# Local block: the feed-forward's layer norm on token rows, with transposes there and back

## The chip, the cores and the metric

The kernel runs on one core of a Trainium2 chip. The metric is the time of one execution on the device, in microseconds (us), the median of several. "Faster" and "slower" mean by over 2%.

## The reference, cut to what matters

The program is a stack of blocks over 4 sequences of 512 tokens with 128 channels. Two of them are the "local transformer" (6 layers each, so 12 layers in all). A layer is windowed attention over 16 heads, and then a feed-forward whose input is layer-normalised over the 128 channels:

```python
def ffn_layer(x, g, bln, W1, b1, W2, b2):
    mu = x.mean(-1, keepdims=True)
    var = ((x - mu) ** 2).mean(-1, keepdims=True)
    xn = (x - mu) / jnp.sqrt(var + 1e-05) * g + bln
    hg = xn @ W1 + b1
    a, gate = jnp.split(hg, 2, -1)
    return a * jax.nn.gelu(gate, approximate=False) @ W2 + b2
for i in range(DEPTH):
    x = attn_layer(shift_tokens(x), Wqkv[i], q_scale[i], k_scale[i], Wo[i]) + x
    x = ffn_layer(shift_tokens(x), ln_g[i], ln_b[i], W1[i], b1[i], W2[i], b2[i]) + x
```

The change touches `mu`, `var` and `xn` of this function alone. All is float32.

## The kernel before

The activations lie with channels on the partitions and tokens along the free axis (`zs`, 128 x 512 for each sequence). A local block (`local_transformer_block`) walks, for each of its 6 layers, over 16 tiles of 128 tokens, four tiles to a sequence. Each engine has its own hand-written list of work, a function `step(L, n, live)`, and the lists meet only in semaphores, so each engine runs strictly in the order of its own `step`. There are 16 steps to a layer, and step n works on several tiles at once: it projects tile n, turns and scores tile n-1, normalises the probabilities of tile n-2, takes the values of tile n-3 and the output projection of tile n-4.

The feed-forward works on a whole sequence, so its pieces come only in some steps. I name a step by n modulo 4. With the last tile of a sequence called t (t modulo 4 is 3), the pieces for that sequence are: `mean` and `centre` in step t+4 (a step 3), `square_centred`, `variance`, `take_variance` and `deviation` in step t+5 (a step 0), `spread`, `rescale`, `affine` and the first `gate` in step t+6 (a step 1), then `gate`/`gelu`/`lin`/`hidden` in steps t+6 to t+9, and `last_matmul` with `add_ffn` in step t+9 (a step 0 again). Step 0 therefore holds pieces of two sequences: the end of one (`hidden(.., 2)`, `last_matmul`, `add_ffn`) and the statistics of the next. There are 4 sequences x 6 layers x 2 blocks = 48 such rounds, and a round lasts four steps.

The eight banks of PSUM are all given out: pairs W, X and Y belong to the attention, and the feed-forward has two single banks, FB and ZB. `gate` and the third `lin` write FB, `gelu` and `hidden(.., 2)` read it; `output`, `mean`, `variance`, the other `lin` and `last_matmul` write ZB.

In the kernel before, the mean over channels is a matmul with a matrix of 1/128, so that it comes out already spread over the partitions; VectorE subtracts it, ScalarE squares, a second set of matmuls sums the squares into token rows, GpSimd takes the inverse root, and a third set of matmuls spreads it back over the partitions, where VectorE multiplies. A float32 matmul shows as two records in the trace; a transpose (L722) shows as one.

## Time and profile before

| what | value |
|---|---|
| median of 3 runs | 4303.71 us (4302.72, 4303.71 and 5915.56) |
| span of the profiled execution | 4291.8 us, 11.9 us under that median |
| TensorE (PE) busy | 4005.3 us, 93% of the span |
| VectorE (DVE) busy | 3375.6 us, 79% |
| GpSimd (POOL) busy | 2963.9 us, 69% |
| ScalarE (ACT) busy | 2587.5 us, 60% |
| a steady stretch of the first local block, 600 to 1960 us | PE 1313.25 of 1360 us, DVE 1191.28, POOL 1183.60, ACT 899.55 |
| granted TensorE clock there | 1.00 |

How to read it: one execution is profiled, and its span runs from the first to the last instruction; its whole time is not given, and the median lies 11.9 us above the span. The third run is far off the two others and plays no part. Busy shares are of the whole span; the local blocks fill about three quarters of it, and there the shares are higher, as the row on the steady stretch shows. A matmul's record ends later than the next one's start, since they are pipelined, so what a group of matmuls costs TensorE is read from start to start.

### The profile page before, as it was taken

What the parts mean: (1) busy time and instruction counts of PE and PEld (TensorE: products, weight loads), DVE (VectorE), ACT (ScalarE), POOL (GpSimd) and SP (SyncE); (2) the same over time, 40 slices, a digit from 0 to 9 for tenths busy, and PEclk for the clock granted to TensorE, in tenths of its full rate; (3) what the DMA queues carried; (4) which work ended last, traced back from release to release, by engine and by line L of the source; (5) the groups of instructions that cost most, each with busy time, mean ns of one, the idle gap of its engine ahead of it and who ended that gap; (6) DMA issues with size and microseconds to landing.
All of it is one profiled execution on the core that took longest, in us unless ns stands there. A gap on an engine that the chain in (4) does not pass through costs nothing. (4 is left out here: it accounts for less than half of the span.)

```text
span 4291.8 us, 151611 instructions
## 1 busy us (share of the span) xinstructions
PE 4005.3 (93%) x66856; PEld 2945.8 (69%) x66856; DVE 3375.6 (79%) x4005; ACT 2587.5 (60%) x3022; POOL 2963.9 (69%) x3505
## 2 busy tenths in 40 slices
PE   8989969999999999999978887799999999999997
PEld 5655557777778778877733333577778787777775
DVE  5636568898888888888668884788898888888885
ACT  4424436666667667666537774467667666666664
POOL 2202158888889888888634440788888888888884
PEclk9999989999999999999989998899999999999999
DMA  4304333232332333322100000323323333232221
GB/s 149 128 10 145 106 95 84 72 93 79 81 89 80 85 79 82 87 75 75 41 11 1 1 1 1 114 80 86 89 74 86 89 85 85 72 90 76 75 64 41
DMA packets 169725, 316.93 MB, mean 74 GB/s; under 512 B 39336, under 2 KB 43056, under 8 KB 166640
## 3 DMA queue, kind: packets, MB, share of 16 engines
q1 hardware_dynamic: 153520, 241.18, 20.7%
q0 software_dynamic: 15552, 66.07, 5.0%
q8 instruction: 529, 8.67, 0.9%
q14 instruction: 124, 1.02, 0.1%
HBM read 92.03 MB, written 20.05 MB: 26 GB/s over the span
## 5 line engine op out<-in xcount | busy, mean ns | idle before, releaser
L715 PE MATMUL psum<-loc_w_hl,loc_z_lo 128*128 128x512 f32 x1152 | 508.1, 441 | 34.3 <-DMA loc_w_hl<-parted 26.6
L1100 POOL TENSOR_TENSOR loc_rc_k<-loc_rc_k,loc_rs_k 128x1024 f32<-128x1024 f32 x192 | 454.5, 2367 | 19.0 <-DVE loc_rs_k L1228 19.0
L1214 DVE TENSOR_REDUCE loc_ssq<-loc_sq 128x16 f32<-128x1024 f32 x384 | 464.1, 1209 | 4.1 <-POOL loc_rn L1096 4.1
L1100 POOL TENSOR_TENSOR loc_rc_q<-loc_rc_q,loc_rs_q 128x1024 f32<-128x1024 f32 x192 | 459.9, 2395 | 0.0
L961 ACT ACTIVATE loc_sq<-psum 128x1024 f32<-128x1024 f32 x192 | 196.9, 1026 | 432.6 <-PE psum L717 427.5
L716 PE MATMUL psum<-loc_w_hl,loc_z_hi 128*128 128x512 f32 x1152 | 454.1, 394 | 2.1 <-issue 2.1
L717 PE MATMUL psum<-loc_w_hl,loc_z_hi 128*128 128x512 f32 x1152 | 455.2, 395 | 0.0
L1118 POOL TENSOR_TENSOR loc_prob<-loc_prob,loc_recip 128x1024 f32<-128x1024 f32 x192 | 365.7, 1905 | 92.5 <-DVE loc_recip L1251 91.7
L812 PE MATMUL psum<-loc_PT,loc_V 64*64 64x32 f32 x24576 | 404.6, 220 | 8.4 <-issue 7.8
L812 PEld LDWEIGHTS psum<-loc_PT,loc_V 64*64 64x64 f32 x24576 | 380.8, 135 | 33.2 <-issue 9.9
L832 PEld LDWEIGHTS psum<-loc_outT,loc_wo 128*128 128x128 f32 x3072 | 375.9, 193 | 17.9 <-issue 1.7
L1106 POOL TENSOR_TENSOR loc_qk_q<-loc_rc_q,loc_rn 128x1024 f32<-128x1024 f32 x192 | 366.0, 1906 | 27.3 <-issue 1.7
L1209 DVE TENSOR_TENSOR loc_rc_q<-psum,loc_rot 128x1024 f32<-128x1024 f32 x192 | 234.5, 1222 | 183.9 <-ACT loc_sq L956 149.7
L832 PE MATMUL psum<-loc_outT,loc_wo 128*128 128x128 f32 x3072 | 377.9, 276 | 0.1
L1106 POOL TENSOR_TENSOR loc_qk_k<-loc_rc_k,loc_rn 128x1024 f32<-128x1024 f32 x192 | 366.9, 1911 | 12.0
L786 PEld LDWEIGHTS psum<-loc_kT,loc_qT 64*32 64x32 f32 x24576 | 270.0, 105 | 125.2 <-issue 123.8
L991 ACT ACTIVATE loc_PT<-psum 128x1024 f32<-128x1024 f32 x192 | 197.0, 1026 | 263.5 <-PE psum L722 263.4
L1544 ACT ACTIVATE full_probT<-psum 128x512 f32<-128x512 f32 x512 | 272.4, 598 | 116.3 <-PE psum L1472 116.3
L786 PE MATMUL psum<-loc_kT,loc_qT 64*32 64x64 f32 x24576 | 309.8, 226 | 34.7 <-issue 34.1
L415 DVE TENSOR_TENSOR moe_hid<-moe_hid,moe_spread 128x512 f32<-128x512 f32 x256 | 217.9, 867 | 154.7 <-ACT moe_hid L329 144.5
L1605 DVE TENSOR_REDUCE full_least<-psum 128x2 f32<-128x1024 f32 x256 | 305.9, 1219 | 19.9 <-PE psum L1465 15.1
L1236 DVE TENSOR_REDUCE loc_negmax<-psum 128x16 f32<-128x1024 f32 x192 | 234.4, 1221 | 90.7 <-PE psum L786 89.6
(201 smaller groups left out, 9731.0 us busy)
## 6 DMA issues: line engine op xcount, KB each, us to landing
loc_V<-loc_V SPq DMA_DIRECT2D x1152, 128.0 KB
loc_V<-loc_V SPq DMA_DIRECT2D x672, 64.0 KB
loc_w_hl<-parted POOLq DMA_DIRECT2D x72, 512.0 KB, 4.3
parted<-moe_halves POOLq DMA_DIRECT2D x18, 1024.0 KB, 5.2
moe_spread<-moe_gates SPq DMA_DIRECT2D x64, 256.0 KB, 4.2
moe_raw<-in_wqkv POOLq DMA_DIRECT2D x18, 512.0 KB, 6.0
moe_w<-in_moe_w SPq DMA_DIRECT2D x32, 256.0 KB, 3.4
loc_wo<-in_wo SPq DMA_DIRECT2D x12, 512.0 KB, 4.8
```

Source lines behind the costliest of these rows:

```text
L715: pe.matmul(M.bank[bank + g], z_lo[:, r, tokens], w[:, 0, cols], start=True, stop=False)
L716: pe.matmul(M.bank[bank + g], z_hi[:, r, tokens], w[:, 1, cols], start=False, stop=False)
L717: mm = pe.matmul(M.bank[bank + g], z_hi[:, r, tokens], w[:, 0, cols], start=False, stop=True)
L786: mm = pe.matmul(M.bank[YB + c][q:q + 32, p * 64:(p + 1) * 64], qT[r:r + 64, p, q:q + 32], kT[r:r + 64, p, k0:k0 + 64], start=False, stop= ...
L812: mm = pe.matmul(M.bank[WB + c][64 * j:64 * j + 64, m * P + q:m * P + q + 32], V2[r:r + 64, b, w, p * 64:(p + 1) * 64], PT[r:r + 64, p, q: ...
L832: mm = pe.matmul(M.bank[ZB][:, 0:P], wo[:, p, :], outT[:, p // (PAIRS // 2), p % (PAIRS // 2), :], start=(p == 0), stop=(p == PAIRS - 1))
L1100: pool.tensor_tensor(rc, rc, rs[:, :], ALU.add).then_inc(added, 1)
L1106: pool.tensor_tensor(pair_major(out[:, :, :, :]), by_pair(rc), spread_heads(rn[:, a:a + HEADS], DH), ALU.mult).then_inc(ready, 1)
L1118: pool.tensor_tensor(both, both, spread_heads(recip[:, :], 2 * WINDOW), ALU.mult).then_inc(p_ready, 1)
L1214: dve.tensor_reduce(ssq[:, a:a + HEADS], heads(sq[:, :]), AX_X, ALU.add).then_inc(totalled, 1)
L1544: act.activation(probT[:, (u * 8 + y * 4 + kb) % SETS, r, :], B[B_BANKS[n % 3]], ACT.Exp).then_inc(b_free, 1)
L1605: dve.tensor_reduce(least[:, u % 2, i, 2 * (k % 2):2 * (k % 2) + 2, y], M.psum[:, b:b + 2, :], AX_X, ALU.max, negate=True).then_inc(a_free, 1)
```

## The change

The norm is taken on token rows. The sequence (four 128 x 128 tiles of `zs`) is transposed by TensorE into bank FB (`turn_rows`, four transposes), so each partition holds one token. VectorE takes mean and variance of each row (`row_statistics`: four `bn_stats` on PSUM, four `bn_aggr`). GpSimd (`deviation`) adds epsilon, negates the mean, takes the inverse root as before and multiplies, three more small instructions than before. ScalarE scales and shifts the rows (`norm_rows`: four 128 x 128 activations from FB to `rows`, scale and bias per partition). TensorE transposes back into ZB (`turn_back`, four transposes), and `affine` on ScalarE reads ZB and not SBUF. Gone are `mean`, `variance` and `spread` on TensorE, `centre`, `take_variance` and `rescale` on VectorE, and `square_centred` on ScalarE.

Some waits of TensorE change with it: `output` and `last_matmul` wait for other, mostly older, events, and `turn_rows` waits for all three `hidden` of the sequence before, because `hidden(.., 2)` reads bank FB.

```diff
...
@@ -586,8 +586,9 @@
-        xc, sqf, xn = sb("xc", [P, T]), sb("sqf", [P, T]), sb("xn", [P, T])
-        var, rstd, vt = (sb(n, [P, TILES]) for n in ("var", "rstd", "vt"))
+        rows, xn = sb("rows", [P, TILES, D]), sb("xn", [P, T])
+        halves, stats = sb("halves", [P, TILES, 6]), sb("stats", [P, TILES, 2])
+        var, rstd, vt, lift = (sb(n, [P, TILES]) for n in ("var", "rstd", "vt", "lift"))
@@ -820,40 +821,36 @@
                 if i == 0:
-                    pe.wait_ge(centred, upto_seq(L, s - 1))
+                    pe.wait_ge(hid_ready, upto_seq(L, s - 2, FBLK) - 1)
                 elif i == 1:
-                    pe.wait_ge(var_ready, upto_seq(L, s - 1))
                     pe.wait_ge(z_ffn, upto_seq(L, s - 2))
                 elif i == 2:
-                    pe.wait_ge(z_attn, upto(L, t - 1))
+                    pe.wait_ge(xn_ready, upto_seq(L, s - 1))
                 else:
                     pe.wait_ge(hid_ready, upto_seq(L, s - 1, FBLK) - 2)
+                pe.wait_ge(z_attn, upto(L, t - 1))
+                pe.sem_inc(pe_passed, 1)
                 for p in range(PAIRS):
...
-            def mean(L, t):
+            def turn_rows(L, t):
+                s = t // TILES
                 pe.wait_ge(z_attn, upto(L, t))
-                pe.wait_ge(hid_ready, upto_seq(L, t // TILES - 1, FBLK) - 1)
-                pe.matmul(M.bank[ZB], M.mean_w[:, :], zs[:, t // TILES % SEQS, 0:T], start=True, stop=True).then_inc(mean_full, 1)
-
-            def variance(L, t, newest):
-                pe.wait_ge(xc_squared, upto_seq(L, t // TILES))
-                pe.wait_ge(z_attn, upto(L, newest))
-                for i in range(TILES):
-                    mm = pe.matmul(M.bank[ZB][:, i * P:(i + 1) * P], sqf[:, i * P:(i + 1) * P], M.mean_w[:, :],
-                                   start=True, stop=True)
-                mm.then_inc(var_full, 1)
-
-            def spread(L, t):
-                s = t // TILES
-                pe.wait_ge(rstd_ready, upto_seq(L, s))
                 pe.wait_ge(hid_ready, upto_seq(L, s - 1, FBLK))
                 for i in range(TILES):
-                    mm = pe.matmul(M.bank[FB][:, i * P:(i + 1) * P], rstd[:, i:i + 1].broadcast_to([P, P]), M.ident[:, :],
-                                   start=True, stop=True)
-                mm.then_inc(spread_full, 1)
+                    mm = pe.transpose(M.bank[FB][:, i * P:(i + 1) * P], zs[:, s % SEQS, i * P:(i + 1) * P], M.ident[:, :])
+                mm.then_inc(rows_full, 1)
+
+            def turn_back(L, t, newest):
+                pe.wait_ge(rows_normed, upto_seq(L, t // TILES))
+                pe.wait_ge(z_attn, upto(L, newest))
+                pe.wait_ge(z_ffn, upto_seq(L, t // TILES - 1))
+                pe.sem_inc(pe_passed, 1)
+                for i in range(TILES):
+                    mm = pe.transpose(M.bank[ZB][:, i * P:(i + 1) * P], rows[:, i, :], M.ident[:, :])
+                mm.then_inc(back_full, 1)
@@ -882,8 +879,7 @@
             def last_matmul(L, t, newest):
...
                     pe.wait_ge(w2_loaded, L * 16 + 16)
-                if newest is not None:
-                    pe.wait_ge(var_ready, upto_seq(L, newest // TILES))
+                pe.wait_ge(z_attn, upto(L, newest))
                 pe.wait_ge(hid_ready, upto_seq(L, t // TILES, FBLK))
@@ -898,15 +894,15 @@
                     values(L, n - 3, live(n - 1))
-                if live(n - 6) and lasts(n - 6):
-                    spread(L, n - 6)
+                if live(n - 5) and lasts(n - 5):
+                    turn_rows(L, n - 5)
                 if live(n - 7) and lasts(n - 7):
...
                     project_q(L, n, live(n - 3))
-                if live(n - 5) and lasts(n - 5):
-                    variance(L, n - 5, newest)
+                if live(n - 6) and lasts(n - 6):
+                    turn_back(L, n - 6, newest)
                 if live(n - 8) and lasts(n - 8):
@@ -919,11 +915,9 @@
                 if live(n - 9) and lasts(n - 9):
-                    last_matmul(L, n - 9, n - 5 if live(n - 5) else None)
+                    last_matmul(L, n - 9, newest)
                 if live(n - 7) and lasts(n - 7):
                     gate(L, n - 7, 2)
-                if live(n - 4) and lasts(n - 4):
-                    mean(L, n - 4)
                 if live(n - 2):
@@ -990,15 +984,18 @@
-            def square_centred(L, t):
-                act.wait_ge(centred, upto_seq(L, t // TILES))
-                act.activation(sqf[:, :], xc[:, :], ACT.Square).then_inc(xc_squared, 1)
+            def norm_rows(L, t):
+                act.wait_ge(norm_ready, upto_seq(L, t // TILES))
+                for i in range(TILES):
+                    done = act.activation(rows[:, i, :], M.bank[FB][:, i * P:(i + 1) * P], ACT.Identity,
+                                          scale=rstd[:, i:i + 1], bias=lift[:, i:i + 1])
+                done.then_inc(rows_normed, 1)
             def affine(L, t):
...
                     act.wait_ge(norm_loaded, L * 16 + 16)
-                act.wait_ge(xn_scaled, upto_seq(L, t // TILES))
-                act.activation(xn[:, :], xn[:, :], ACT.Identity, scale=vec[:, 2 * FBLK + 1:2 * FBLK + 2],
+                act.wait_ge(back_full, upto_seq(L, t // TILES))
+                act.activation(xn[:, :], M.bank[ZB], ACT.Identity, scale=vec[:, 2 * FBLK + 1:2 * FBLK + 2],
                                bias=vec[:, 2 * FBLK + 2:2 * FBLK + 3]).then_inc(xn_ready, 1)
@@ -1011,8 +1008,6 @@
             def step(L, n, live):
...
                     copy_probs(L, n - 3)
-                if live(n - 5) and lasts(n - 5):
-                    square_centred(L, n - 5)
                 if live(n - 7) and lasts(n - 7):
@@ -1025,6 +1020,8 @@
                     gelu(L, n - 8, 2)
+                if live(n - 6) and lasts(n - 6):
+                    norm_rows(L, n - 6)
                 if live(n):
@@ -1127,18 +1124,24 @@
             def deviation(L, t):
                 s = t // TILES
-                step = L * (SEQS * 4) + s * 4
-                pool.wait_ge(var_ready, upto_seq(L, s))
+                step = L * (SEQS * 7) + s * 7
+                pool.wait_ge(stats_ready, upto_seq(L, s))
+                pool.tensor_scalar(var[:, :], stats[:, :, 1], LN_EPS, None, ALU.add).then_inc(rstd_step, 1)
+                pool.tensor_scalar(lift[:, :], stats[:, :, 0], -1.0, None, ALU.mult).then_inc(rstd_step, 1)
+                pool.wait_ge(rstd_step, step + 2)
+                pool.sem_inc(pool_passed, 1)
                 pool.tensor_tensor(rstd[:, :], var[:, :], minus_half[:, 0:TILES], ALU.pow).then_inc(rstd_step, 1)
-                pool.wait_ge(rstd_step, step + 1)
+                pool.wait_ge(rstd_step, step + 3)
                 pool.tensor_tensor(vt[:, :], rstd[:, :], rstd[:, :], ALU.mult).then_inc(rstd_step, 1)
-                pool.wait_ge(rstd_step, step + 2)
+                pool.wait_ge(rstd_step, step + 4)
                 pool.tensor_tensor(vt[:, :], vt[:, :], var[:, :], ALU.mult).then_inc(rstd_step, 1)
-                pool.wait_ge(rstd_step, step + 3)
+                pool.wait_ge(rstd_step, step + 5)
                 pool.sem_inc(pool_passed, 1)
                 pool.tensor_scalar(vt[:, :], vt[:, :], -0.5, 1.5, ALU.mult, ALU.add).then_inc(rstd_step, 1)
-                pool.wait_ge(rstd_step, step + 4)
-                pool.tensor_tensor(rstd[:, :], rstd[:, :], vt[:, :], ALU.mult).then_inc(rstd_ready, 1)
+                pool.wait_ge(rstd_step, step + 6)
+                pool.tensor_tensor(rstd[:, :], rstd[:, :], vt[:, :], ALU.mult).then_inc(rstd_step, 1)
+                pool.wait_ge(rstd_step, step + 7)
+                pool.tensor_tensor(lift[:, :], lift[:, :], rstd[:, :], ALU.mult).then_inc(norm_ready, 1)
@@ -1258,18 +1261,15 @@
-            def centre(L, t):
+            def row_statistics(L, t):
                 s = t // TILES
-                dve.wait_ge(mean_full, upto_seq(L, s))
-                dve.tensor_tensor(xc[:, :], zs[:, s % SEQS, 0:T], M.bank[ZB], ALU.subtract).then_inc(centred, 1)
-
-            def take_variance(L, t):
-                dve.wait_ge(var_full, upto_seq(L, t // TILES))
-                dve.tensor_scalar(var[:, :], M.bank[ZB].rearrange("p (i n) -> p i n", n=P)[:, :, 0], LN_EPS, None, ALU.add).then_inc(var_ready, 1)
-
-            def rescale(L, t):
-                dve.wait_ge(spread_full, upto_seq(L, t // TILES))
-                dve.tensor_tensor(xn[:, :], xc[:, :], M.bank[FB], ALU.mult).then_inc(xn_scaled, 1)
+                dve.wait_ge(rows_full, upto_seq(L, s))
+                for i in range(TILES):
+                    dve.bn_stats(halves[:, i, :], M.bank[FB][:, i * P:(i + 1) * P]).then_inc(row_stats, 1)
+                for i in range(TILES):
+                    dve.wait_ge(row_stats, (L * SEQS + s) * TILES + i + 1)
+                    mv = dve.bn_aggr(stats[:, i, :], halves[:, i, :])
+                mv.then_inc(stats_ready, 1)
@@ -1314,13 +1314,11 @@
                     add_attention(L, n - 4)
-                if live(n - 6) and lasts(n - 6):
-                    rescale(L, n - 6)
                 if live(n - 2):
...
                 if live(n - 5) and lasts(n - 5):
-                    take_variance(L, n - 5)
+                    row_statistics(L, n - 5)
                 if live(n - 8) and lasts(n - 8):
@@ -1330,8 +1328,6 @@
                     hidden(L, n - 7, 0)
-                if live(n - 4) and lasts(n - 4):
-                    centre(L, n - 4)
                 if live(n):
...
```

The places where the order moves, all in the first local block. In them `psum` is any bank of PSUM, `loc_gg` the gated hidden values, `loc_outT`/`loc_wo` the output projection, `loc_PT`/`loc_V` the values.

TensorE, step 0, around the values of the attention; before:

```order
L832 MATMUL psum<-loc_outT,loc_wo 128x128 x8
L812 MATMUL psum<-loc_PT,loc_V 64x32 x64
L715 MATMUL psum<-loc_w_hl,loc_z_lo 128x512
L716 MATMUL psum<-loc_w_hl,loc_z_hi 128x512
L717 MATMUL psum<-loc_w_hl,loc_z_hi 128x512
```

and now:

```order
L834 MATMUL psum<-loc_outT,loc_wo 128x128 x8
L813 MATMUL psum<-loc_PT,loc_V 64x32 x64
L843 MATMUL psum<-ident,zs 128x128 x4
L716 MATMUL psum<-loc_w_hl,loc_z_lo 128x512
L717 MATMUL psum<-loc_w_hl,loc_z_hi 128x512
L718 MATMUL psum<-loc_w_hl,loc_z_hi 128x512
```

Four transposes of `zs` stand between the values (L812, now L813) and the projection of v; the four `variance` matmuls, which stood behind the projection of q, are gone.

VectorE, step 0, from the sine product of k (L1228, now L1231) over `hidden(.., 2)` (`loc_gg`) to the cosine product of q; before:

```order
L1228 TENSOR_TENSOR loc_rs_k<-psum,loc_rot 128x1024
L1279 SCALAR_TENSOR_TENSOR loc_gg<-psum,loc_vec,loc_gg 85x512
L1256 TENSOR_TENSOR zs<-zs,psum 64x128
L1258 TENSOR_TENSOR zs<-zs,psum 64x128
L1246 TENSOR_REDUCE loc_total<-loc_prob 128x16
L1251 RECIPROCAL loc_recip<-loc_total 128x16
L1268 TENSOR_SCALAR loc_var<-psum 128x4
L1209 TENSOR_TENSOR loc_rc_q<-psum,loc_rot 128x1024
```

and now:

```order
L1231 TENSOR_TENSOR loc_rs_k<-psum,loc_rot 128x1024
L1279 SCALAR_TENSOR_TENSOR loc_gg<-psum,loc_vec,loc_gg 85x512
L1259 TENSOR_TENSOR zs<-zs,psum 64x128
L1261 TENSOR_TENSOR zs<-zs,psum 64x128
L1249 TENSOR_REDUCE loc_total<-loc_prob 128x16
L1254 RECIPROCAL loc_recip<-loc_total 128x16
L1268 BN_STATS loc_halves<-psum 128x6 x4
L1271 BN_AGGR loc_stats<-loc_halves 128x2 x4
L1212 TENSOR_TENSOR loc_rc_q<-psum,loc_rot 128x1024
```

Eight small instructions stand where `take_variance` stood, behind the reciprocal and ahead of the cosine product of q.

ScalarE, step 1, around the copy of the attention's result (`loc_outT`); before:

```order
L961 ACTIVATE loc_sq<-psum 128x1024
L987 ACTIVATE loc_prob<-loc_prob 128x1024
L982 ACTIVATE loc_outT<-psum 128x1024
L968 ACTIVATE loc_V<-psum 128x1024
L956 ACTIVATE loc_sq<-psum 128x1024
L1001 ACTIVATE loc_xn<-loc_xn,loc_vec 128x512
L977 ACTIVATE loc_kT<-psum 128x8x128
L972 ACTIVATE loc_qT<-psum 128x1024
```

and now:

```order
L955 ACTIVATE loc_sq<-psum 128x1024
L981 ACTIVATE loc_prob<-loc_prob 128x1024
L976 ACTIVATE loc_outT<-psum 128x1024
L990 ACTIVATE loc_rows<-psum,loc_lift,loc_rstd 128x128 x4
L962 ACTIVATE loc_V<-psum 128x1024
L950 ACTIVATE loc_sq<-psum 128x1024
L998 ACTIVATE loc_xn<-psum,loc_vec 128x512
L971 ACTIVATE loc_kT<-psum 128x8x128
L966 ACTIVATE loc_qT<-psum 128x1024
```

Four activations stand between the copy of `loc_outT` and the copy of `loc_V`; `affine` (`loc_xn`) keeps its place and reads `psum`.

## Rows read from the trace of the kernel before

**Rows 1.** The profile's page: busy us of each engine, share of the span, instructions.
```profile
PE 4005.3 (93%) x66856; PEld 2945.8 (69%) x66856; DVE 3375.6 (79%) x4005; ACT 2587.5 (60%) x3022; POOL 2963.9 (69%) x3505
```

**Rows 2.** Windows of a steady stretch: length, then busy us (instructions) by engine, clock, DMA.
```profile
600.00:1960.00 1360.00, 1313.25 (x27412) 1066.27 (x27412) 1191.28 (x1364) 899.55 (x917) 1183.60 (x1445) 1.00 0.31 82
```

**Rows 3.** Timeline of TensorE, steps 3 and 0: start, duration, engine, line, operation, [idle before].
```profile
1201.59 1.02 PE L839 MATMUL psum<-zs,mean_w 128*128 128x512 f32 x2
1202.44 1.04 PE L722 MATMUL psum<-ident,loc_prob 128*128 128x128 f32 x8
...
1208.62 2.07 PE L812 MATMUL psum<-loc_PT,loc_V 64*64 64x32 f32 x128
1210.62 0.50 PE L715 MATMUL psum<-loc_w_hl,loc_z_lo 128*128 128x512 f32 x1
...
1213.49 1.05 PE L845 MATMUL psum<-mean_w,loc_sqf 128*128 128x128 f32 x8
1214.38 1.04 PE L722 MATMUL psum<-ident,loc_qk_k 128*128 128x128 f32 x8
1215.25 1.04 PE L722 MATMUL psum<-ident,loc_qk_q 128*128 128x128 f32 x8
```

**Rows 4.** Timeline of VectorE, the same step 0.
```profile
1205.49 1.23 DVE L1236 TENSOR_REDUCE loc_negmax<-psum 128x16 f32<-128x1024 f32 x1 [0.51 <-PE psum L786]
...
1211.41 0.74 DVE L1279 SCALAR_TENSOR_TENSOR loc_gg<-psum,loc_vec,loc_gg 85x512 f32<-85x512 f32 x1
...
1213.92 0.25 DVE L1251 RECIPROCAL loc_recip<-loc_total 128x16 f32<-128x16 f32 x1
1214.58 0.16 DVE L1268 TENSOR_SCALAR loc_var<-psum 128x4 f32<-128x4 f32 x1 [0.40 <-PE psum L845]
```

**Rows 5.** Timeline of TensorE, the step 1 that follows.
```profile
1226.89 1.16 PE L854 MATMUL psum<-ident,loc_rstd 128*128 128x128 f32 x8
1227.80 0.48 PE L715 MATMUL psum<-loc_w_hl,loc_z_lo 128*128 128x512 f32 x1
...
1232.71 1.10 PE L866 MATMUL psum<-loc_xn,loc_w 128*128 128x512 f32 x2 [0.16 <-ACT loc_xn L1001]
1233.65 1.04 PE L722 MATMUL psum<-ident,loc_prob 128*128 128x128 f32 x8
```

**Rows 6.** Timeline of ScalarE, the same step 1.
```profile
1227.03 1.02 ACT L982 ACTIVATE loc_outT<-psum 128x1024 f32<-128x1024 f32 x1 [1.83 <-PE psum L812]
1229.48 1.03 ACT L968 ACTIVATE loc_V<-psum 128x1024 f32<-128x1024 f32 x1 [1.43 <-PE psum L717]
...
1231.77 0.80 ACT L1001 ACTIVATE loc_xn<-loc_xn,loc_vec 128x512 f32<-128x512 f32 x1
1232.47 1.01 ACT L977 ACTIVATE loc_kT<-psum 128x1024 f32<-128x1024 f32 x1
```

**Rows 7.** Timeline of GpSimd, from step 0 into step 1.
```profile
1218.52 1.05 POOL L1132 TENSOR_TENSOR loc_rstd<-loc_var,loc_minus_half 128x4 f32<-128x4 f32 x1
...
1220.77 0.24 POOL L1075 TENSOR_TENSOR loc_rt<-loc_rn 128x32 f32<-128x32 f32 x1
...
1230.88 1.91 POOL L1118 TENSOR_TENSOR loc_prob<-loc_prob,loc_recip 128x1024 f32<-128x1024 f32 x1
```

**Rows 8.** Groups by line, whole run: busy us, mean ns | idle us before them.
```profile
L1241 DVE TENSOR_TENSOR loc_prob<-psum,loc_negmax 128x1024 f32<-128x1024 f32 x192 | 235.1, 1225 | 6.6
...
L972 ACT ACTIVATE loc_qT<-psum 128x1024 f32<-128x1024 f32 x192 | 197.3, 1028 | 22.7 <-PE psum L722 22.5
...
L1264 DVE TENSOR_TENSOR loc_xc<-zs,psum 128x512 f32<-128x512 f32 x48 | 33.0, 687 | 3.6 <-PE psum L839 3.0
...
L1562 ACT ACTIVATE full_plain<-psum,sel 128x512 f32<-128x512 f32 x32 | 22.0, 688 | 5.3 <-PE psum L1489 4.5 <-DVE full_qkk L1622 0.8
...
L1560 ACT ACTIVATE full_plain<-psum 128x512 f32<-128x512 f32 x16 | 9.6, 598 | 34.1 <-PE psum L1489 34.1
```

**Rows 9.** One line's instructions, whole run: duration ns min/median/max.
```profile
L1219 DVE TENSOR_SCALAR loc_ssq<-loc_ssq x192: 169/836/2049, 581.9 to 4218.6; 128x32 f32<-128x32 f32 x192
```

More of the change, by code:

```diff
@@ L549, in local_transformer_block @@
         root_ready = sem("root_ready")
-        mean_full, var_full, spread_full, gate_full, lin_full, ffn_full = (
-            sem(n) for n in ("mean_full", "var_full", "spread_full", "gate_full", "lin_full", "ffn_full"))
-        xc_squared, xn_ready, gelu_done = (sem(n) for n in ("xc_squared", "xn_ready", "gelu_done"))
-        centred, var_ready, xn_scaled, hid_ready, z_ffn = (
-            sem(n) for n in ("centred", "var_ready", "xn_scaled", "hid_ready", "z_ffn"))
-        rstd_step, rstd_ready = sem("rstd_step"), sem("rstd_ready")
+        rows_full, back_full, gate_full, lin_full, ffn_full = (
+            sem(n) for n in ("rows_full", "back_full", "gate_full", "lin_full", "ffn_full"))
+        rows_normed, xn_ready, gelu_done = (sem(n) for n in ("rows_normed", "xn_ready", "gelu_done"))
+        row_stats, stats_ready, hid_ready, z_ffn = (
+            sem(n) for n in ("row_stats", "stats_ready", "hid_ready", "z_ffn"))
+        rstd_step, norm_ready = sem("rstd_step"), sem("norm_ready")
         v2_loaded = [sem(f"v2_loaded_{i}") for i in range(TILES)]
@@ L942, in _ @@
         def _(act):
-            for one in (qT_ready, kT_ready, q_squared, k_squared, exp_done, v_ready, pt_ready, outT_ready, xc_squared, xn_ready):
+            for one in (qT_ready, kT_ready, q_squared, k_squared, exp_done, v_ready, pt_ready, outT_ready, rows_normed, xn_ready):
                 act.sem_inc(one, CREDIT)
@@ L1052, in _ @@
             for one in (tq_full, tk_full, q_full, k_full, v_full, y_full, s_full, pt_full, pv_full, q_ready, k_ready,
-                        mean_full, var_full, spread_full, ffn_full, rstd_ready):
+                        rows_full, back_full, ffn_full, norm_ready):
                 pool.sem_inc(one, CREDIT)
```

2 lines of the change are left out of this document (1 added, 1 removed).

## The prediction

> **What bounds the kernel now.** I first read the page: TensorE is busy 93% of the span, the others 60 to 79% [rows 1]. That is a mean over stages, so next comes one steady stretch of a local block, the only kind of stage that the change touches: there TensorE is busy 1313.25 of 1360 us at a granted clock of 1.00, VectorE 1191.28, GpSimd 1183.60 [rows 2]. So TensorE is the bound, with 46.75 us idle (3.4%), and VectorE and GpSimd fill 87% and so can become it in a single step. Then I read one round of four steps in the timelines, each instruction's start against the one that it waits for: TensorE's step 3 and step 0 [rows 3], VectorE in that step 0 [rows 4], TensorE and ScalarE in step 1 [rows 5, 6], and GpSimd from one to the other [rows 7]. There are 48 rounds.
>
> What TensorE's work costs is read from start to start, since its records overlap.
>
> **The change on TensorE, in work alone.** Removed in each round: `mean`, 1202.44 - 1201.59 = 0.85 us in step 3 [rows 3]; `variance`, 1214.38 - 1213.49 = 0.89 us in step 0 [rows 3]; `spread`, 1227.80 - 1226.89 = 0.91 us in step 1 [rows 5]. Added: two groups of four transposes. Eight transposes of k take 1215.25 - 1214.38 = 0.87 us, so four take 0.44 [rows 3]; the record of the eight, 1.04 us long and halved, is the upper bound, 0.52. Work saved: 0.85 + (0.89 - 0.44) + (0.91 - 0.44) = 1.77 us a round, 85 us in all. If nothing else moved, the kernel would gain that.
>
> **The wait that comes in step 0.** `turn_rows` stands right behind the values, and waits for `hidden(.., 2)` of the sequence before. In this step 0 the values give way to the projection of v at 1210.62 [rows 3], but VectorE runs `hidden(.., 2)` from 1211.41 to 1212.15 [rows 4]. Nothing can make it earlier: it is the sixth in a chain of VectorE that starts when the scores of the step before end (maximum at 1205.49, with 0.51 us idle before it, waiting for them) and runs on without a break (maximum, subtraction, cosine, squares, sine, hidden), 6.66 us, while TensorE's own work from the same scores to the values' end is shorter. Both sides start from the scores, so taking work out of step 3 moves both and not their distance. The wait is 1212.15 - 1210.62 = 1.53, with 0.05 for the semaphore 1.58 us. It falls in 46 of the 48 rounds, since the first sequence of each block has none before it: 46 x 1.58 = 72.7 us. Behind the waiting `turn_rows` stand both projections, and for them wait ScalarE's copy of v and square of q, and VectorE's cosine. In the kernel before, only `last_matmul`, 5 us later, waited for the same event, and never had to. The other altered waits cost nothing: `output` now waits for `affine`, which `gate` a step before has waited for already, for a `hidden` of the sequence before the last, and for its own predecessor's addition.
>
> **VectorE.** Out: `centre` and `rescale` (0.69 us each [rows 8]) in steps 3 and 1, where it has slack, and `take_variance`, 0.16 in step 0 [rows 4]. In, in step 0: four `bn_stats` and four `bn_aggr`, which no row shows. The lower bound is 0.16 us each, as the smallest read of PSUM [rows 4], 1.3 us in all. For `bn_stats` on 128 columns I take the line through 1225 ns for 1024 and 687 ns for 512 columns, 1.05 ns a column, so 0.28 us [rows 8]; upper bound 0.69, the price of 512 columns. For `bn_aggr` I take the reciprocal's 0.25 [rows 4], upper bound 0.30. Taken: 4 x 0.28 + 4 x 0.25 = 2.1 us; upper bound 4.0. The cover: VectorE's next work, the cosine of q, needs ScalarE's square of q, and that comes late now. TensorE leaves the wait at 1212.20, the transposes end at 1212.64, the projections (1213.49 - 1210.62 = 2.87 us) at 1215.51, the square 0.2 + 1.03 us later, at 1216.74. The reciprocal ends at 1214.17. So 2.57 us are covered, the 2.1 us cost nothing, and the upper bound costs 1.4 x 46 = 64 us.
>
> **GpSimd.** `deviation` takes 1220.77 - 1218.52 = 2.25 us [rows 7] and gets three instructions more; with one wait between them I take 1.0 us (0.6 to 1.4). Behind it stands the root for q and k (starting 1220.77), and at the end of that chain the probabilities, 1230.88 + 1.91 = 1232.79, for which `turn_probs` of step 1 waits. It started at 1233.65 [rows 5], 0.86 us later. Step 0 grows by 1.58 + 0.44 - 0.89 = 1.13 us, so GpSimd's 1.0 us is hidden by the very wait above. Without that wait it would show.
>
> **ScalarE, step 1.** The chain that ends the step's middle is its own: copy of the result (1227.03), copy of v, square of q, `affine`, copy of kT, at 1233.48 [rows 6], and `turn_probs` at 1233.65 follows it. In: four activations of 128 columns. From 1028 ns for 1024 and 598 for 512 columns it is 0.84 ns a column, so 0.28 us, plus 0.09 for a scale or bias read per partition (688 against 598): 0.37 us each, 1.5 us [rows 8]; upper bound 0.69 each, 2.75 us. ScalarE is idle for 1.43 us at just that place [rows 6], waiting for the projection of v, which now comes 0.47 us earlier. `affine` goes from 0.80 us to 0.69 as it reads PSUM [rows 6, 8]. So the chain ends about 1.43 - 1.5 + 0.11 = 0.04 us earlier by whole records; by starts, each record overlaps the next by 0.1 us, which gives back 0.4 us. TensorE would allow 0.47, and GpSimd's probabilities cap it in the rounds where they are already last. I take a gain of 0.3 us a round, 14.4 us in all, between +0.47 and -1.0 (-23 to +48 us). `square_centred` is gone from a place where ScalarE was idle: nothing.
>
> The Trainium skill (VectorE: DVE Perf Modes, section on the TRN2 errata) says that VectorE and ScalarE pay a fixed cost for every instruction, and advises tiles of 512 elements and more; it speaks against four activations of 128 where one of 512 would do. The rows agree (4 x 0.28 = 1.1 against 0.60 us), and by the rule's advice the sum loses 0.5 us of ScalarE's time a round, which the idle 1.43 us takes up.
>
> **The sum.** Step 3: -0.85 x 48 = -40.8. Step 0: -0.45 x 48 + 72.7 = +51.1. Step 1: -14.4. Together -4.1 us. At the end of each block, where nothing overlaps, the old chain of small pieces and the new one have about the same length: 0 +- 3. The profiled execution's span of 4291.8 becomes 4287.7; with the 11.9 us around it, which I leave as they are, and against the median of 4303.7: **4300 us**. A measurement of this kernel can tell about 2% (86 us) from no change.
>
> **The rivals.**
> - *As forecast, the wait eats the saving*: 0.55, with 4280 to 4325 as its own range.
> - *The work saved comes back in full*: 4303.7 - 85 = 4219, up to 10 us less if step 1 gives more (4209). For it: TensorE is the bound. Against it: two timelines that start from the same event. 0.08.
> - *Part comes back*: the pause of TensorE lets the other engines catch up, and takes the place of idle time that is there anyway (46.75 us in 21 rounds, 2.2 us a round [rows 2]). If 0.9 us of each round's were so replaced: 4300 - 43 = 4257. 0.13.
> - *GpSimd becomes the bound in step 1*: its 1.0 us is not hidden, because its chain doesn't move with TensorE's wait: 4300 + 48 = 4348. It has 0.86 us of room in the round shown. 0.14.
> - *Slower by more than the bound: the statistics wait for GpSimd.* One small VectorE instruction on SBUF, 128 x 32, takes from 169 to 2049 ns, 836 in the middle [rows 9], though its work never changes: it stretches while a GpSimd instruction runs. If `bn_aggr`, which also reads and writes SBUF, is held in the same way, it waits out the GpSimd instruction of that moment, 1.9 us at most by that spread. Held once, the eight take 2.1 + 1.9 = 4.0 us against a cover of 2.57: 4300 + 46 x 1.4 = 4364. Held a second time, behind the next GpSimd instruction: 5.9 us, 4300 + 46 x 3.3 = 4452. It passes 2% from 4.5 us on. Against it: the reciprocal, as small and on SBUF too, took 0.25 there [rows 4]. 0.07.
> - *The change doesn't do what it says*, or another event of the altered waits bites: 0.03.
>
> The Trainium skill (Perfetto Trace Analysis, section "Optimizing Scalar/DVE Operations") gives a reason for the last but one: GpSimd shares VectorE's second port to SBUF, and a VectorE instruction that uses both ports holds it alone. The spread of 169 to 2049 ns agrees. It doesn't say whether `bn_aggr` is such an instruction.
>
> **Range and chances.** 4250 to 4350 takes in the first, third and fourth case, 0.82. Faster by over 2% means under 4218: a part of the second case, 0.04. Slower by over 2%, above 4390: a part of the fifth and of the sixth, 0.05. Within 2%: 0.91.
>
> **What the profile after will show.** Right if: the first transpose of `turn_rows` has 1.5 to 1.6 us idle before it, released by VectorE's `loc_gg`; `bn_stats` near 0.28 and `bn_aggr` near 0.25 us, with the cosine of q behind them still waiting for ScalarE's square; `norm_rows` near 0.37 us each; `deviation` about 3.2 us from its first start to the root's; TensorE's work less by 1.77 us a round and its idle time more by as much. Wrong if `turn_rows` has under 1 us of idle time, if the cosine of q follows `bn_aggr` without a gap, or if `turn_probs` of step 1 waits for GpSimd in most rounds.

## The result, and the profile after

The changed kernel took 4332.35 us, median of 6 runs (4331.16 to 4342.22), beside 4314.89 for the kernel before on the same chip: ratio **1.0055** (95% interval 1.0035 to 1.0075). The run of 5915.56 us has no part in the ratio, and the quotient of the two medians, 1.0040, lies inside the interval. In a second comparison (e13 below) it was 1.0102 (1.0075 to 1.0130). By the two ratios it is slower by 24 and 44 us; the forecast was 4 us less than before. The page of its profiled execution (4342.22 us), engines and TensorE's granted clock:

```profile
span 4340.4 us, 151415 instructions
...
PE 3963.0 (91%) x66376; PEld 2913.2 (67%) x66376; DVE 3328.5 (77%) x4245; ACT 2611.2 (60%) x3166; POOL 2994.0 (69%) x3649
...
PEclk9999989999999999999979997899999999999999
```

TensorE has less to do than in [rows 1], and the span is 48.6 us longer. That overstates the difference: a span lies 1.8 us under its run's time here (4340.4 and 4342.22) and 1.9 in e0 below (4310.3 and 4312.19), so the profiled execution of before, 4291.8 us, was itself some 10 us faster than its median run. The 11.9 us that the prediction put around the span are mostly this.

Most of the two local blocks as windows, first of the kernel after, then of the kernel before (length, busy us of PE, PEld, DVE, ACT, POOL, granted clock, DMA share, GB/s):

```profile
560.00:2110.00 1550.00, 1439.47 (x29904) 1169.98 (x29907) 1286.62 (x1627) 1004.19 (x1080) 1326.84 (x1671) 0.97 0.31 82
2670.00:4340.00 1670.00, 1526.38 (x31090) 1223.53 (x31082) 1332.11 (x1718) 1042.61 (x1132) 1359.91 (x1719) 0.96 0.29 77
```

```profile
560.00:2090.00 1530.00, 1461.22 (x30331) 1184.97 (x30334) 1326.65 (x1523) 998.01 (x1017) 1318.54 (x1615) 0.99 0.31 83
2640.00:4292.00 1652.00, 1553.77 (x31334) 1245.05 (x31332) 1345.56 (x1599) 1031.29 (x1062) 1344.64 (x1647) 0.98 0.29 78
```

The windows are 20 and 18 us longer, TensorE's idle time in them grows, and the clock column falls from 0.99 and 0.98 to 0.97 and 0.96. Now one step 0 of the kernel after, TensorE's timeline, to be held against [rows 3]:

```profile
1213.09 2.07 PE L813 MATMUL psum<-loc_PT,loc_V 64*64 64x32 f32 x128
1216.75 0.63 PE L843 MATMUL psum<-ident,zs 128*128 128x128 f32 x4 [1.59 <-DVE loc_gg L1279]
1217.13 0.48 PE L716 MATMUL psum<-loc_w_hl,loc_z_lo 128*128 128x512 f32 x1
...
1219.97 1.03 PE L723 MATMUL psum<-ident,loc_qk_k 128*128 128x128 f32 x8
```

The forecast wait is there: 1.59 us, released by VectorE's `hidden`. VectorE behind it (against [rows 4]), GpSimd's deviation (against [rows 7]) and ScalarE in the step 1 that follows (against [rows 6]):

```profile
1217.13 1.22 DVE L1249 TENSOR_REDUCE loc_total<-loc_prob 128x16 f32<-128x1024 f32 x1
1218.38 0.25 DVE L1254 RECIPROCAL loc_recip<-loc_total 128x16 f32<-128x16 f32 x1
1218.67 0.89 DVE L1268 BATCH_NORM_STATS2 loc_halves<-psum 128x6 f32<-128x128 f32 x4
1219.48 0.36 DVE L1271 BATCH_NORM_AGGREGATE loc_stats<-loc_halves 128x2 f32<-128x6 f32 x4
1221.23 1.22 DVE L1212 TENSOR_TENSOR loc_rc_q<-psum,loc_rot 128x1024 f32<-128x1024 f32 x1 [1.39 <-ACT loc_sq L950]
```

```profile
1223.04 0.22 POOL L1129 TENSOR_SCALAR loc_var<-loc_stats 128x4 f32<-128x4 f32 x1
...
1223.75 1.05 POOL L1133 TENSOR_TENSOR loc_rstd<-loc_var,loc_minus_half 128x4 f32<-128x4 f32 x1 [0.18 <-POOL loc_lift L1130]
```

```profile
1233.55 1.50 ACT L990 ACTIVATE loc_rows<-psum,loc_lift,loc_rstd 128x128 f32<-128x128 f32 x4
1234.91 1.05 ACT L962 ACTIVATE loc_V<-psum 128x1024 f32<-128x1024 f32 x1
```

The eight statistics take 1.17 us (1219.48 + 0.36 - 1218.67), and the cosine of q still waits 1.39 us for ScalarE behind them: the cover holds. The root follows the deviation at 1226.27, 3.23 us after 1223.04.

**Where the time went.** Of each local block I take the steady part, from step n = 9 of its first layer to the last layer's n = 14: 172 steps in the two blocks, 42 of them steps 0. From the records there: length, TensorE's idle time by what ended it, and the time at the lower of the clock's two levels (1.2 GHz, against 2.4), half of which I count as lost. "Work" is busy time less that half. "Issue" is idle time that the profile puts down to nothing. Gaps under 0.15 us (3.3 and 1.5 us in all) stand in no row.

| us, steady parts | before | after | after less before |
|---|---|---|---|
| length | 2765.0 | 2799.2 | +34.2 |
| work | 2692.8 | 2616.0 | -76.8 |
| idle behind VectorE's `hidden` and others | 3.7 | 59.1 | +55.4 |
| idle behind GpSimd, ScalarE | 15.2 | 8.3 | -6.9 |
| idle, "issue" | 44.8 | 75.5 | +30.7 |
| half the time at the lower clock | 5.1 (of 10.2) | 38.9 (of 77.8) | +33.8 |

The first two changes were forecast, and leave a gain of 21.4 us together. The last two were not, and make the kernel slower. The second profile of the changed kernel (e13) has a steady part of 2813.0 us, 13.8 more than this one, so a difference of single profiles is good to some 15 us; its "issue" (75.4) is the same, its lower clock a little more (88.7).

The clock: 22 stretches at the lower level lie whole in the steady part of after (a 23rd is cut by its end), 3 in that of before; a second profile of each had 26 and 2. Next to the start of 12 of the 22 stands the wait of step 0, and to that of the other 10 an "issue" pause of 1.7 to 2.4 us; in 7 of the 22 the pause still lasts, for up to 0.41 us, when the stretch begins. One such place in the kernel after, TensorE's timeline, and the window over it (columns as above):

```profile
1737.35 0.64 PE L843 MATMUL psum<-ident,zs 128*128 128x128 f32 x4 [1.60 <-DVE loc_gg L1279]
...
1739.06 0.63 PE L716 MATMUL psum<-loc_w_hl,loc_z_lo 128*128 128x512 f32 x1
1739.49 0.63 PE L717 MATMUL psum<-loc_w_hl,loc_z_hi 128*128 128x512 f32 x1
...
1741.46 0.40 PE L716 MATMUL psum<-loc_w_hl,loc_z_lo 128*128 128x512 f32 x1
1741.69 0.40 PE L717 MATMUL psum<-loc_w_hl,loc_z_hi 128*128 128x512 f32 x1
```

```profile
1737.90:1741.20 3.30, 3.30 (x10) 2.53 (x10) 2.46 (x10) 0.62 (x1) 2.71 (x3) 0.50 0.00 0
```

After the wait, matmuls start 0.43 us apart (1739.49 - 1739.06) instead of 0.23 (1741.69 - 1741.46), at a granted clock of 0.50. TensorE shows as fully busy there, so no idle time tells of it: only the clock column does. Whether the half really lengthens the kernel can be read inside a profile, from steps with and without such a stretch. A straight-line fit of the steps' lengths (a constant for each of the four steps, "issue" idle time, and this half) gives 0.94 us of length for each us so counted in e3 below (+- 0.05), 0.98 in e13 (+- 0.07), but 0.64 (+- 0.07) in the profile of after: there the 38.9 us may be nearer 25.

### The profile page after: what moved, and what is told of

It reads as the page before. It is cut to its first block and busy times, and to the rows that moved or that the text cites. A ratio compares the mean times of both kernels' runs of the same rounds, so it can differ in the third digit from the quotient of the medians.

```text
span 4340.4 us, 151415 instructions
## 1 busy us (share of the span) xinstructions
PE 3963.0 (91%) x66376; PEld 2913.2 (67%) x66376; DVE 3328.5 (77%) x4245; ACT 2611.2 (60%) x3166; POOL 2994.0 (69%) x3649
## 3 DMA queue, kind: packets, MB, share of 16 engines
q1 hardware_dynamic: 153520, 241.18, 20.5%
## 5 line engine op out<-in xcount | busy, mean ns | idle before, releaser
L716 PE MATMUL psum<-loc_w_hl,loc_z_lo 128*128 128x512 f32 x1152 | 518.6, 450 | 40.1 <-DMA loc_w_hl<-parted 24.8
L717 PE MATMUL psum<-loc_w_hl,loc_z_hi 128*128 128x512 f32 x1152 | 464.2, 403 | 4.1 <-issue 4.1
L718 PE MATMUL psum<-loc_w_hl,loc_z_hi 128*128 128x512 f32 x1152 | 463.2, 402 | 1.0 <-issue 1.0
L813 PE MATMUL psum<-loc_PT,loc_V 64*64 64x32 f32 x24576 | 407.9, 220 | 13.9 <-issue 13.1
L813 PEld LDWEIGHTS psum<-loc_PT,loc_V 64*64 64x64 f32 x24576 | 383.2, 135 | 41.2 <-issue 17.5
L1103 POOL TENSOR_TENSOR loc_qk_k<-loc_rc_k,loc_rn 128x1024 f32<-128x1024 f32 x192 | 367.4, 1914 | 11.9
L1601 DVE TENSOR_REDUCE full_least<-psum 128x2 f32<-128x1024 f32 x256 | 305.8, 1219 | 20.2 <-PE psum L1461 15.2
L976 ACT ACTIVATE loc_outT<-psum 128x1024 f32<-128x1024 f32 x192 | 196.9, 1025 | 177.9 <-PE psum L813 177.9
```

Source lines behind the costliest of these rows:

```text
L716: pe.matmul(M.bank[bank + g], z_lo[:, r, tokens], w[:, 0, cols], start=True, stop=False)
L717: pe.matmul(M.bank[bank + g], z_hi[:, r, tokens], w[:, 1, cols], start=False, stop=False)
L718: mm = pe.matmul(M.bank[bank + g], z_hi[:, r, tokens], w[:, 0, cols], start=False, stop=True)
L813: mm = pe.matmul(M.bank[WB + c][64 * j:64 * j + 64, m * P + q:m * P + q + 32], V2[r:r + 64, b, w, p * 64:(p + 1) * 64], PT[r:r + 64, p, q: ...
L1103: pool.tensor_tensor(pair_major(out[:, :, :, :]), by_pair(rc), spread_heads(rn[:, a:a + HEADS], DH), ALU.mult).then_inc(ready, 1)
L1601: dve.tensor_reduce(least[:, u % 2, i, 2 * (k % 2):2 * (k % 2) + 2, y], M.psum[:, b:b + 2, :], AX_X, ALU.max, negate=True).then_inc(a_free, 1)
```

## The experiments

Ratios are to the kernel before on the same chip, with 95% intervals. "In 42 rounds" and the tables below mean the steady part.

**e0, the kernel before again.** 

> The kernel before, unchanged, so that its trace comes from the same chip as those of the experiments. Every theory: ratio 1.000 +- 0.003. The clock theory: in the steady parts of the two local blocks the granted clock stays at its upper level almost everywhere (3 dips in the first trace), mean clock near 0.977. Rival (the chip, not the change, makes the dips): as many dips as in the changed kernel (25), mean clock near 0.965.

Measured: 0.9993 (0.9976 to 1.0009), with 2 stretches at the lower clock, so this chip by itself doesn't make them. The steady part took 2766.8 us against 2765.0, with 49.9 us of "issue" against 44.8 and 6.8 us at the lower clock: a row of "issue" repeats to about 5 us.

**e1, the turning taken behind the wait's reach.**

```
                 (step 0, ahead of project_v)
-                if live(n - 5) and lasts(n - 5):
-                    turn_rows(L, n - 5)
...
                 (behind project_q)
+                if live(n - 5) and lasts(n - 5):
+                    turn_rows(L, n - 5)
```

> The changed kernel, turn_rows moved from ahead of the projections of v and q to behind them, so that hidden(.., 2) has long ended when TensorE comes to it. Theory (the wait costs 1.58 us x 46 = 73 us, and the pause it makes costs another 40 us or so through the granted clock): no idle time before the transposes, few dips of the clock; but the statistics lose their cover of 2.57 us, and VectorE lengthens step 0 by about 1 us: before - 85 + 46 = ratio 0.991 (0.980 to 0.995). Rival (statistics, GpSimd or ScalarE make the change slow, the clock only goes along): no better than the changed kernel, ratio 1.005 or more.

Measured: 0.9946 (0.9931 to 0.9961). The wait is gone, but 73.0 us of idle behind GpSimd are there. TensorE in step 1:

```profile
1231.22 1.04 PE L723 MATMUL psum<-ident,loc_qk_k 128*128 128x128 f32 x8
...
1233.87 1.09 PE L723 MATMUL psum<-ident,loc_qk_q 128*128 128x128 f32 x8 [1.61 <-POOL loc_qk_q L1103]
```

and GpSimd, which runs from the deviation's start at 1220.37 through the root (its last piece below) to the end of q at 1233.81 with no pause longer than 0.2 us:

```profile
1227.18 0.25 POOL L1093 TENSOR_TENSOR loc_rn<-loc_rn,loc_rt 128x32 f32<-128x32 f32 x1
1227.51 1.91 POOL L1103 TENSOR_TENSOR loc_qk_k<-loc_rc_k,loc_rn 128x1024 f32<-128x1024 f32 x1
1229.37 2.40 POOL L1097 TENSOR_TENSOR loc_rc_q<-loc_rc_q,loc_rs_q 128x1024 f32<-128x1024 f32 x1
1231.91 1.90 POOL L1103 TENSOR_TENSOR loc_qk_q<-loc_rc_q,loc_rn 128x1024 f32<-128x1024 f32 x1
```

So the rival of the prediction in which GpSimd becomes the bound in step 1 is real, and the wait of step 0 had hidden it. The ratio is as expected, but not by the way that was expected: VectorE did not lengthen step 0 (16.02 us in the middle, without a low clock, against 16.32 in e0), GpSimd lengthened step 1 (16.22 against 15.61). "Issue" idle time is back at 44.3 us, and the lower clock at 34.1, in 10 stretches; 7 of the 10 follow one of the new waits for GpSimd, of 1.9 to 2.2 us.

**e2 and e4, the wait shortened in two other ways.** e2 lets VectorE run `hidden(.., 2)` first in its step; e4 puts the turning between the two projections.

> The changed kernel, turn_rows where it is; instead VectorE runs hidden(.., 2) first in its step 0, ahead of the cosine of k, so that it ends some 1.5 us before TensorE asks for it. Theory (once the wait is gone, GpSimd's longer chain is the next bound, and it holds TensorE at the turning of q in step 1 by 1.5 us): no idle time before the transposes of zs, 1.3 to 1.7 us before the turning of q in step 1, ratio 0.995 (0.991 to 0.998), as with turn_rows moved. Rival (the wait alone held the kernel, and moving turn_rows had a cost of its own): ratio 0.985 or less.

> The changed kernel, turn_rows between the projections of v and q: 1.37 us of real work ahead of the wait, which leaves about 0.2 us of it. Theory of GpSimd's chain as next bound: 0.2 us idle before the transposes, 1.2 to 1.6 us before the turning of q in step 1, ratio 0.995 (0.991 to 0.998). Rival (the wait alone): ratio 0.985 or less.

Measured: 0.9967 (0.9952 to 0.9983) and 0.9974 (0.9958 to 0.9990), with GpSimd's idle at 66.7 and 61.3 us, as the theory had it. Three ways to take the wait away (e1, e2, e4) give the same picture: 10, 10 and 11 stretches at the lower clock in place of 22 and 26, and 44.3, 46.3 and 48.9 us of "issue" in place of 75.5 and 75.4.

**e3, the wait alone, put into the kernel before.**

```
+                if live(n - 5) and lasts(n - 5):
+                    pe.wait_ge(hid_ready, upto_seq(L, (n - 5) // TILES - 1, FBLK))
+                    pe.sem_inc(pe_passed, 1)
                 (behind the values, ahead of project_v in step 0)
```

> The kernel before, with nothing but the wait of turn_rows put at its place: behind the values of step 0, TensorE waits for hidden(.., 2) of the sequence before. Clock theory: 46 x 1.58 = 73 us of waiting and some 25 dips of the clock, up to 1.7 us each, 37 us: +110 us, ratio 1.025 (1.020 to 1.028). Wait alone, no clock: +73 us, ratio 1.017. Rival (the pause is absorbed by slack elsewhere): under +30 us, ratio below 1.007.

Measured: 1.0227 (1.0207 to 1.0247). Its steady part is 106.6 us longer than before: 62.4 of idle behind VectorE, 34.1 from the lower clock (78.5 us of it, 10.2 before), 11.6 more "issue" (6.5 more than in e0). A wait that shows as 62 us of idle costs 107. So the bare wait makes the whole clock part of the changed kernel (33.8 us), but only a part of its 30.7 us of "issue". TensorE's groups in e3, whole run:

```profile
L715 PE MATMUL psum<-loc_w_hl,loc_z_lo 128*128 128x512 f32 x1152 | 517.9, 450 | 97.9 <-DVE loc_gg L1282 64.6 <-DMA loc_w_hl<-parted 26.4 <-DVE loc_rs_q L1231 2.8
```

**e8 and e5, the wait filled with work.** A projection of v whose result is thrown away (6 matmuls of 512 columns) stands ahead of the waiting place, in e8 on top of e3, in e5 on top of the changed kernel.

```
...
+                    if live(n):
+                        thrown_away(L, n, live(n - 2))
                     (ahead of the wait for hid_ready in step 0)
```

> The kernel before with the added wait, and the wait filled: ahead of it TensorE computes the projection of v once more and throws it away. The step is as long as with the wait alone, only the pause is gone. Clock theory (a pause of 1.5 us in step 0 makes the dips of the clock, half of whose time is lost): dips in step 0 gone, and 25 to 35 us faster than with the bare wait (1.0227), so 1.015 to 1.017, unless pauses of TensorE's instruction supply grow as they did when the wait of the changed kernel was filled; then the clock's part shows in the sum over the steady steps: busy time less half of the time at the lower clock stays the same plus 42 x 1.37 = 58 us. Rival (dips cost nothing): 1.023 or more with unchanged pauses.

> The changed kernel, with the wait filled: ahead of turn_rows in step 0 TensorE computes the projection of v once more (six matmuls, 1.37 us) and throws it away; the true one follows as before. Nothing becomes shorter by it. Clock theory: idle time before the transposes falls from 1.59 to 0.2 us, the dips of the clock go back from 25 to a few, and the kernel gets about 35 to 40 us faster than the changed one: ratio to the kernel before 0.996 (0.993 to 0.999). Rival (the clock has no part in it): the same as the changed kernel, 1.005, or slower if the 1.37 us don't fit into the wait.

Measured: e8 1.0219 (1.0189 to 1.0248), e5 1.0105 (1.0086 to 1.0124).

| us, steady parts | e3 | e8 | after | e5 |
|---|---|---|---|---|
| work | 2691.3 | 2763.2 | 2616.0 | 2683.0 |
| idle behind VectorE | 66.1 | 2.6 | 59.1 | 0.4 |
| "issue" | 56.4 | 65.6 | 75.5 | 107.8 |
| at the lower clock | 78.5 | 23.1 | 77.8 | 50.5 |

e8 is not faster than e3 by its ratio, where the theory had 1.015 to 1.017: the steady part is 7.6 us shorter. The fill adds 71.9 us of work (from start to start it took TensorE 70.7 us, 1.68 a time, and not the 1.37 expected) and takes 63.5 of idle away; "issue" grows by 9.2 us. With TensorE at work in that place the lower clock falls by 55.4 us, worth 27.7: from 1.38 us a step 0 in e3 to none at all, while in the other steps it stays (20.5 and 23.1 us). That ties the lower clock to the idle time and not to this place in the step; the total alone, with a fill dearer than the pause, could not show it. In e5 the stretches in step 0 went as well (1.63 to 0.24 us a step 0), but "issue" grew by 32.3 us and the lower clock in the other steps with it, and the fill added 67.0 us against 58.7 of idle taken away: e5 came out slower than the changed kernel, not faster as the theory had it.

**e6, e11, e9 and e12, GpSimd's deviation shortened.** The Newton step is left out of the deviation (8 instructions to 4; in the kernel before 5 to 1), which changes the layer norm's precision: e6 on top of e1, e11 on the kernel before, e9 and e12 (the same kernel twice) on the changed one.

```
-                pool.tensor_tensor(vt[:, :], rstd[:, :], rstd[:, :], ALU.mult).then_inc(rstd_step, 1)
...
-                pool.tensor_scalar(vt[:, :], vt[:, :], -0.5, 1.5, ALU.mult, ALU.add).then_inc(rstd_step, 1)
-                pool.wait_ge(rstd_step, step + 6)
-                pool.tensor_tensor(rstd[:, :], rstd[:, :], vt[:, :], ALU.mult).then_inc(rstd_step, 1)
```

> As with turn_rows behind the projections, and GpSimd's deviation cut from 8 instructions to 4: the refinement of the inverse root (one Newton step, left out) is gone, about 1.2 to 1.3 us of its 3.2. Theory (GpSimd's chain is the bound in step 1): the idle time before the turning of q in step 1 falls from 1.6 to about 0.4 us, and the kernel gains 46 x 1.2 = 55 us on the one without the cut: ratio 0.982 (0.978 to 0.987). Rival (the chain only rides along, VectorE's step 0 sets the pace): no change, 0.9946.

> The kernel before with the Newton step alone left out: how much of the gain of e6 the cut gives by itself. Theory (TensorE is bound in the kernel before, and waits for GpSimd 11 to 14 us in 42 rounds): 0.998 (0.995 to 1.000). Rival (GpSimd's length costs time everywhere): 0.988 or less.

> The changed kernel, turn_rows in its place with its wait for hidden(.., 2); the deviation is cut from 8 instructions of GpSimd to 4 (the Newton step is left out). Theory (the wait of 1.4 us per round in step 0 hides GpSimd's longer step): as the changed kernel, 1.0055 (1.003 to 1.007), with TensorE's idle time behind VectorE's hidden unchanged at about 59 us in 42 rounds. Rival (GpSimd's length already sets the end in the changed kernel, the wait or not): 0.993 or less, as e6 stands 0.0115 under e1.

> The kernel of e9 once more, whose profile can't be read: the changed kernel with GpSimd's deviation in 4 instructions instead of 8. It came out at 1.0109, slower than the changed kernel, which neither theory had. Theory (the shorter step of GpSimd lets TensorE reach the wait of step 0 earlier, and stand there longer: the wait gives back what step 1 saves, and the granted clock falls in step 0 as before): 1.006 to 1.013, TensorE's idle time behind VectorE's hidden over 65 us in 42 rounds, against 59. Rival (a disturbance of e9 alone): 1.0055 as the changed kernel, the idle time at 59 us or less.

> The changed kernel itself, on the same chip as e12, as its yardstick: 1.0055 (1.0035 to 1.0075), with some 20 stretches of the lower granted clock in the steady part of the two local blocks. Rival (the stretches are an accident of one profile): fewer than 8 of them.

Measured: e6 **0.9831** (0.9794 to 0.9869), e11 1.0009 (0.9996 to 1.0022), e9 1.0109 (1.0086 to 1.0133; its profiled execution took 10694 us and is not read), e12 1.0149 (1.0122 to 1.0176) beside e13, the changed kernel, 1.0102 (1.0075 to 1.0130).

The same cut is worth 1.2% once the wait is gone (e1 to e6: idle behind GpSimd 73.0 to 21.8 us), and nothing in the kernel before. In the changed kernel it saves nothing, and rather costs: on the same chip the four runs of e12 (4363 to 4372 us) all lie above the four of e13 (4335 to 4353). Neither theory of e9 had that. The theory of e12 fails too: its wait did not grow (54.6 us, 62.8 in e13), and its ratio is above the range given; and e9 was no accident, against the rival. What grew is "issue", 75.4 to 110.5 us, with the lower clock at 88.7 us in both. e13 itself lies above its expected range, with the many stretches that were expected, 26: the two comparisons of the changed kernel differ by nearly all that their intervals allow (they meet at 1.0075), and why is open.

**e7 and e10, GpSimd's issues of weight loads moved out of steps 0 and 1.** e7 on top of e1, e10 on top of e6.

```
-                if n in (3, 5) and L + 1 < DEPTH:
+                if n in (3, 6) and L + 1 < DEPTH:
...
-                if n in (8, 10) and L + 1 < DEPTH:
+                if n in (7, 10) and L + 1 < DEPTH:
...
-                if n in (12, 14) and L + 1 < DEPTH:
+                if n in (11, 14) and L + 1 < DEPTH:
```

> The kernel of e1 with GpSimd's issues of weight loads moved out of steps 0 and 1 of a round (to the positions 6, 7 and 11 of their lists); what is computed stays. Theory (in e1 GpSimd ends last in step 1: 73 us of TensorE's idle time in 42 rounds wait for its RoPE of k and q): the idle time ahead of the turning of q in step 1 falls by 0.3 to 0.6 us in the rounds whose loads were issued there, and the ratio to the kernel before goes from 0.9946 to about 0.991 (0.988 to 0.994). Rival (it is what VectorE and ScalarE hand to GpSimd that comes late, not GpSimd's own length): the idle time and the ratio stay, 0.9946.

> e6 (the turning behind project_q, no Newton step) with the weight loads of e7 moved too. Theory (GpSimd's length is what is left: 21.8 us of idle in 42 rounds): about 0.980 (0.976 to 0.984). Rival (what is left is TensorE's own work): as e6, 0.983.

Measured: e7 0.9927 (0.9910 to 0.9943), e10 **0.9787** (0.9763 to 0.9810). The intervals overlap those of e1 and e6, and GpSimd's idle moved only from 73.0 to 67.7 and from 21.8 to 18.7 us: not told apart from no gain. By the medians e7 is the fastest kernel that computes all that the changed one does; e10, without the Newton step, is 2.1% faster than the kernel before (1.9 to 2.4).

**The "issue" pauses: read, not tried.** The page lists DMA queues for instructions, and I take q8 for TensorE's, as its count fits (below). The page of after, and the queues in 1 us at 1400.6:

```profile
q8 instruction: 526, 8.62, 0.9%
```

```profile
q1 hardware_dynamic: 122, 0.19, 73.8%
q8 instruction: 1, 0.02, 5.9%
```

and TensorE's timeline there:

```profile
1399.51 1.32 PE L787 MATMUL psum<-loc_kT,loc_qT 64*32 64x64 f32 x108
1402.92 0.41 PE L787 MATMUL psum<-loc_kT,loc_qT 64*32 64x64 f32 x20 [2.10 <-issue]
1403.26 0.76 PE L716 MATMUL psum<-loc_w_hl,loc_z_lo 128*128 128x512 f32 x1
```

The page counts 526 packets of 16 KB for 66376 matmuls and as many weight loads, one per 252 instructions. The packet in this window landed at 1401.57, and TensorE went on 1.35 us later, in the middle of the scores. So it is with the others: all 37 "issue" pauses over 0.9 us in the steady part of after end 1.22 to 1.60 us behind the landing of such a packet, and the 20 of the kernel before 1.26 to 1.56, while these packets mostly land 4 to 10 us apart. By this reading TensorE had run out of instructions. The packets that ended the 37 pauses landed 9.2 us behind the one before them in the middle, the others 5.1, with hardly more time in transfer (1.25 us against 1.08). In e13, e12, e5 and e1 a few such pauses (4, 6, 4 and 5) lie 3 to 7 us behind a landing and are something else. Pauses over 0.9 us number 20 and 25 in the two profiles of before, 37 and 38 in those of after, 24 in e1, 22 in e10, 53 in e5 and in e12. Why the same stream runs dry more often where TensorE waits in step 0 of the changed kernel, or GpSimd is quick there too, or with a fill, is open: no run changed the stream alone, and no cause of it is shown.

## Why the prediction was wrong, step by step

- **TensorE's work: right.** Forecast 1.77 us a round; 76.8 us in 42 rounds is 1.83.
- **The wait: right in place, cause and size.** Forecast 1.58 us; 1.59 in the round shown, 59.1 / 42 = 1.41 on average. The 0.05 us for the semaphore in it stand in no row: in that round `hidden` ends at 1216.60 and the transposes start 0.15 us later. e1, e2 and e4 removed the wait, e3 made it.
- **Its price: the step that failed.** "The wait that comes in step 0" was priced as its idle time alone, 72.7 us. e3 shows the same wait at 107 us for 62 of idle: a third of the price is the lower clock, and a little is "issue". The prediction read a clock of 1.00 in [rows 2] and kept it, though the change put a pause of 1.6 us into a stretch that had next to none. No rival had this mechanism. In the steady parts the sum's terms come to -0.8 us (-0.85, +1.13 and -0.3 us in each of 42 rounds), and +34.2 were measured, with 33.8 us of clock and 30.7 of "issue" that the sum had at nothing; a shorter wait and a better step 1 give part of that back. That both come with the wait is shown, since both go with it in e1, e2 and e4. That the clock falls at such pauses is seen in the rows. Why it falls only at some, and how the wait brings the "issue" time, of which e3's bare wait made only 6.5 to 11.6 us, stays open.
- **VectorE: hidden, as forecast, and cheaper.** `bn_stats` 280 ns by record (forecast 0.28), `bn_aggr` 148 ns (forecast 0.25), and the eight took 1.17 us and not 2.1, since the records of these small instructions overlap as well. The rival in which the statistics wait for GpSimd did not occur: over the whole run `bn_stats` took 278 to 300 ns and `bn_aggr` 143 to 165.
- **GpSimd: right.** Forecast 3.2 us, measured 3.23; hidden by the wait, as said, and showing without it (e1, 73.0 us).
- **ScalarE: the four activations as priced** (1.5 us; record 1.50, start to start 1.36). Step 1 gave more than the 0.3 us forecast: of steps without a low clock, the median is 14.77 us, against 15.61 in e0. Steps 3 and 0 moved by -0.74 and +1.18 (forecast -0.85 and +1.13), step 2 by +0.08. Summed, an undisturbed round is 0.32 us shorter than before; the mean round, with clock and pauses, is 0.80 longer (65.15 against 64.35). The Trainium skill (VectorE: DVE Perf Modes, section on the TRN2 errata) speaks against small instructions of ScalarE for their fixed cost, with instructions that read SBUF in view; these four read PSUM, and the cost is there too, 1.36 us against 0.60 for one of 512 columns [rows 8]. ScalarE's slack took it up.
- **GpSimd as the bound in step 1** (0.14) was the right mechanism for the kernels without the wait, at 1.6 us in the round shown instead of 1.0.

## What to carry to other kernels

A new wait on the engine that is the bound costs more than its idle time: look up the granted clock of the stretch and what pauses there are, and give a pause of 1.5 us every 65 us a surcharge (here 107 us for 62, in e3). Where a change adds a wait and work behind it, the wait hides the work; take the wait away and look for what it hid before counting the gain: here 77 us less work gave 0.5%, and 1.2% more only when GpSimd's chain was cut too. A cut that is worth nothing beside one bound can be worth a per cent beside another (e11, e6).
